# Three mixing products at once, the fourth beside the fifth: the merged loop of a cross-attention and RWKV layer

## The chip, the core and the metric

One core of a Trainium2 chip runs the whole program. The metric is the device time of one execution in microseconds. A profiled execution gives, beside its time, a trace with the start and the duration of each instruction on the engines TensorE (PE), VectorE (DVE), ScalarE (ACT), GpSimd (POOL) and on the queue of SyncE (SP).

## What is computed

The input is x, 64 sequences of 64 rows with 256 channels, and an encoder state of the same shape. First comes a transformer layer (self-attention, cross-attention, MLP), then an RWKV block on its output. All in float32. The part around the change is the token mixing of the RWKV block, cut to what matters:

```python
sx = concatenate([state[:, 1:2] - xa[:, :1], xa[:, :-1] - xa[:, 1:]], axis=1)
xxx = tanh((xa + sx * maa_x) @ maa_w1).reshape(b, l, 5, 32)
xxx = einsum('blfd,fde->blfe', xxx, maa_w2)            # the five mixing products
xm = xa[:, :, None] + sx[:, :, None] * (maa_stack + xxx)
xk, xw, xv, xr, xg = (xm[:, :, j] for j in range(5))
w = exp(-exp(time_decay + tanh(xw @ td_w1) @ td_w2))
r, k, v, g = xr @ Wr.T, xk @ Wk.T, xv @ Wv.T, silu(xg @ Wg.T)
# then for each step t, per head:  out = r (u * k v + s);  s = k v + w s
```

Each of the five mixing products has a contraction of only 32 (`DM`), so it fills a quarter of TensorE's rows.

## The kernel before

The rows are cut into 16 runs of 256 (`RUNS`, `RT`). The late phase is one merged loop over s: in the turn s, TensorE, VectorE, ScalarE and GpSimd each go through a fixed, hand-written order (their `body(s, u)`), in which several stages of different runs stand side by side. Run s is in the recurrence (states, scan, read), run s + 1 in the mixing and its projections, run s + 2 in the first norm, run s + 3 in the transformer's MLP (`up`, `gelu`, `down`), runs s - 1 and s - 2 in the norm of the heads and the output projection. Turns -2 to 3 are written out, 4 to 11 run as a loop on each engine, 12 to 15 are written out again. From s = 13 on there is no MLP run, and two runs of the channel mix (`ch_...`) a turn take its place. The engines meet only at semaphores; each engine works through its own order and a wait holds up all that stands behind it.

The lines around the change:

- TensorE: `mixer` makes the inputs of the five products, ScalarE's `mixer` takes the tanh of them into `mixer_a` (four products, 32 rows each) and `mixer_b` (the fifth, for two column halves, in rows 0 to 31 and 64 to 95). `mix_pair(r, 0)` (matmul on line 1048) makes products 0 and 1 in the banks `even` and `odd`, side by side since they use different rows. After `up(s + 3, 2)` and `up(s + 3, 3)` (line 999), `mix_pair(r, 2)` makes products 2 and 3 in the same banks, once VectorE has read 0 and 1 (`mixed_ready`). `mix_last` (line 1059) makes the fifth, its two column halves side by side in 64 rows each, half of them zeros. `decay` (line 1101) follows it. `project` (lines 1070 for NW, 1089 for the others) makes the projections in the order NW, NV, NK, NR, NG; NW, NV and NG use the bank `proj`, which `up` uses as well; so NW waits until all GELU activations (line 1387) have read it. NK has `k_bank` and NR `r_bank`, which VectorE reads straight from PSUM up to the end of its turn: `project(s, NR)` is the first step of TensorE's turn and waits for VectorE's last `read` (line 1799).
- `sum_heads` (line 1128) sums the heads in `o_bank`, which `add_heads` on VectorE copies out (`o_copied`).
- VectorE: eight groups n = 0 to 7 a turn, each `key_values` (line 1774), `scan` (1788) and `read` (1799; for n = 2 and 3 on GpSimd, line 903). Between them stand the other steps, the mixing among them: `mix(s + 1, m)` (line 1754, two instructions each) takes product m out of PSUM, for m = 0 and 1 after the scan of n = 3, for 2 and 3 after `centre` at n = 4, for 4 after `sum_squares` (line 1837) at n = 5. Product m goes into one of two buffers `mixed`, m modulo 2, so mix m waits until GpSimd has taken mix m - 2 (`xm_ready`).
- GpSimd: `mix(s + 1, m)` (line 894) adds xa to it; in its order stand the reads of n = 2 and 3, mix 0, mix 1, the MLP's bias (`add_mlp_bias`, line 870), mix 2, mix 3, mix 4, then `scale` (line 911).

## Time and profile before

| | us |
|---|---|
| median of 3 runs | 1121.56 |
| lowest and highest | 1116.63, 1121.56 |
| profiled execution, its own time | 1118.86 |
| its span, first to last instruction | 1117.1 |
| mean granted TensorE clock | 0.989 of full |

| engine | busy us | share of the span |
|---|---|---|
| TensorE (PE) | 1061.3 | 95% |
| its weight loads (PEld) | 883.5 | 79% |
| VectorE (DVE) | 916.1 | 82% |
| ScalarE (ACT) | 702.6 | 63% |
| GpSimd (POOL) | 608.1 | 54% |

The attention takes the first 480 us or so, the merged loop the time from there to about 1060. A busy share is a mean over both. A float32 matmul shows as two instructions, so a product of 128x256 counts as x2. TensorE's records overlap: the next one starts before the end of the last, so its time is read from start to start. A duration on VectorE or GpSimd contains the time for which the instruction had been started and yet stood.

### The profile page before, as it was taken

To read this page: it belongs to the slowest core of one execution; us is meant where nothing else is said; L and a number is where in the kernel's file an instruction comes from. 1 tells how busy PE (TensorE), PEld (TensorE's weight loads), DVE (VectorE), ACT (ScalarE), POOL (GpSimd) and SP (SyncE) were. 2 spreads that over 40 slices of the span, in tenths; PEclk is the share of its full clock that TensorE was granted. 3 is DMA by queue.
4 is the path that set the end of the run, shared out by engine and by line. 5 is a ranking of instruction groups with operands and counts; after the bars stand their busy time and mean duration, and the time that the engine had idled before them with its cause. 6 is when DMAs were issued, how large, how long until landed. Compare 5 with 4: busy or idle time off the path is not lost.

```text
span 1117.1 us, 34410 instructions
## 1 busy us (share of the span) xinstructions
PE 1061.3 (95%) x12992; PEld 883.5 (79%) x12992; DVE 916.1 (82%) x1662; ACT 702.6 (63%) x1606; POOL 608.1 (54%) x535
## 2 busy tenths in 40 slices
PE   5999999999999998999999999999999998788898
PEld 4888988888889887777787877777777776566687
DVE  5997777888777776228999999999999999999753
ACT  5678878777777775465556555456555455544574
POOL 4787887877887885024443454443454443444233
PEclk9999999999999998999999999999999999998999
DMA  8500000011111110013333331233331233304011
GB/s 328 174 4 2 0 0 2 3 41 41 41 48 38 38 47 3 1 28 68 79 83 86 85 70 40 64 81 84 84 76 40 56 82 86 85 10 114 20 38 57
DMA packets 39867, 65.01 MB, mean 58 GB/s; under 512 B 4384, under 2 KB 26208, under 8 KB 39392
## 3 DMA queue, kind: packets, MB, share of 16 engines
q1 hardware_dynamic: 39776, 63.75, 21.4%
q8 instruction: 62, 1.02, 0.4%
q14 instruction: 29, 0.24, 0.1%
HBM read 55.35 MB, written 8.39 MB: 57 GB/s over the span
## 4 chain that ended last, share of the span: by engine, by line
PE 60%; DVE 27%; issue 7%; ACT 3%; DVEq 1%; DMA 1%; SPq 0%; POOL 0%; ACTq 0%; POOLq 0%
PE psum L353 9%; DVE shared L1788 9%; PE psum L267 5%; PE psum L999 5%; PE psum L336 5%; PE psum L1008 4%; PE psum L368 4%; PE psum L1089 4%; DVE shared L1774 4%; PE psum L297 4%; PE psum L280 3%; DVE late_mixed L1754 3%; PE psum L1270 2%; PE psum L310 2%; PE psum L1300 2%
## 5 line engine op out<-in xcount | busy, mean ns | idle before, releaser
L1788 DVE TENSOR_TENSOR_SCAN shared<-late_wT,shared 128x512 f32<-128x512 f32 x128 | 192.4, 1503 | 0.0
L232 POOL TENSOR_TENSOR shared<-shared,att_row_max 128x512 f32<-128x512 f32 x128 | 132.3, 1051 | 17.9 <-DVE att_row_max L564 17.9
L353 PE MATMUL psum<-shared 128*128 128x128 f32 x1024 | 126.6, 277 | 0.0
L453 ACT ACTIVATE shared<-shared 128x512 f32<-128x512 f32 x128 | 80.5, 631 | 67.7 <-POOL shared L232 67.6
L353 PEld LDWEIGHTS psum<-shared 128*128 128x128 f32 x1024 | 121.0, 194 | 0.3 <-ACT shared L462 0.2
L999 PE MATMUL psum<-late_glnT,w 128*128 128x256 f32 x512 | 119.5, 387 | 1.8 <-ACT late_glnT L1378 1.8
L1008 PE MATMUL psum<-w,late_hT 128*128 128x256 f32 x512 | 120.0, 383 | 1.0 <-ACT late_hT L1387 0.9
L564 DVE TENSOR_REDUCE att_row_max<-shared 128x8 f32<-128x512 f32 x128 | 86.9, 680 | 40.9 <-POOL shared L225 40.9
L903 POOL TENSOR_TENSOR shared<-shared,late_rT 128x512 f32<-128x512 f32 x32 | 40.7, 1273 | 140.6 <-DVE shared L1788 140.6
L894 POOL TENSOR_TENSOR late_xm<-late_mixed,late_xa 128x512 f32<-128x512 f32 x64 | 79.7, 1255 | 59.9 <-DVE late_mixed L1754 56.3
L999 PEld LDWEIGHTS psum<-late_glnT,w 128*128 128x128 f32 x512 | 95.8, 192 | 17.9 <-issue 2.8
L1008 PEld LDWEIGHTS psum<-w,late_hT 128*128 128x128 f32 x512 | 94.6, 190 | 15.0 <-ACT late_hT L1387 1.8
L225 POOL TENSOR_TENSOR shared<-shared 128x512 f32<-128x512 f32 x64 | 80.0, 1271 | 41.2 <-DVE shared L557 39.5
L225 POOL TENSOR_TENSOR shared<-shared,self_bias 128x512 f32<-128x512 f32 x64 | 80.2, 1275 | 30.7 <-DVE shared L557 30.7
L1387 ACT ACTIVATE late_hT<-psum,cols 128x256 f32<-128x256 f32 x128 | 53.7, 470 | 65.5 <-PE psum L999 65.1
L1774 DVE TENSOR_TENSOR shared<-shared,psum 128x504 f32<-128x504 f32 x128 | 85.6, 670 | 5.7 <-ACT shared L1431 5.6
L267 PEld LDWEIGHTS psum<-shared 64*64 64x64 f32 x4096 | 65.7, 135 | 21.0 <-issue 20.9
L1754 DVE SCALAR_TENSOR_TENSOR late_mixed<-psum,cols,late_sx 128x256 f32<-128x256 f32 x160 | 66.5, 475 | 15.2 <-PE psum L1048 8.3
L462 ACT ACTIVATE shared<-psum 128x512 f32<-128x512 f32 x128 | 68.4, 585 | 7.8 <-PE psum L280 7.8
L267 PE MATMUL psum<-shared 64*64 64x17 f32 x4096 | 72.1, 209 | 0.0
L424 ACT ACTIVATE shared<-psum,cols 128x256 f32<-128x256 f32 x128 | 65.3, 564 | 9.7 <-PE psum L310 6.8
L336 PE MATMUL psum<-shared 128*128 128x128 f32 x512 | 70.3, 282 | 0.4 <-issue 0.4
(168 smaller groups left out, 2420.9 us busy)
## 6 DMA issues: line engine op xcount, KB each, us to landing
shared<-v_rows SPq DMA_DIRECT2D x64, 512.0 KB, 7.1
shared<-in_enc SPq DMA_DIRECT2D x64, 128.0 KB, 2.6
v_rows<-shared SPq DMA_DIRECT2D x64, 64.0 KB, 1.8
out<-x SPq DMA_DIRECT2D x16, 256.0 KB, 2.0
x<-in_x SPq DMA_DIRECT2D x7, 512.0 KB, 9.7
w<-in_w SPq DMA_DIRECT2D x2, 1024.0 KB, 16.9
shared<-in_cross_mask SPq DMA_DIRECT2D x1, 1024.0 KB, 11.4
shared<-in_w_qkv SPq DMA_DIRECT2D x1, 768.0 KB, 4.5
```

Source lines behind the costliest of these rows:

```text
L225: nc.gpsimd.tensor_tensor(zs, zs, bias.unsqueeze(1).to_broadcast([P, PAIRS, S]), ALU.add).then_inc(biased, 1)
L232: nc.gpsimd.tensor_tensor(zs, zs, peak.unsqueeze(2).to_broadcast([P, PAIRS, S]), ALU.subtract).then_inc(shifted, 1)
L267: last = nc.tensor.matmul(out_banks[e ^ b][rows, pair * 32:pair * 32 + HD + 1], zT[keys, pair, rows], values[keys, u, e ^ b, pair, :], sta ...
L336: last = nc.tensor.matmul(vv[:, e * P:(e + 1) * P].rearrange("p (r d) -> p r d", d=HD), KV[k][:, u % 2, kb, e * S:e * S + P], wv[:, kb, v0 ...
L353: last = nc.tensor.matmul(dst[:, half * P:(half + 1) * P], w[:, kb, c0 + half * P:c0 + (half + 1) * P], src[:, u % 2, kb, 0:P], start=(kb ...
L453: nc.scalar.activation(probs[:, u % 2, half * 4:(half + 1) * 4, :].rearrange("p r k -> p (r k)"), z[:, u % 2, half, :], ACT.Exp).then_inc( ...
L564: nc.vector.tensor_reduce(out=row_max[:, u % 2, half * PAIRS:(half + 1) * PAIRS], in_=z[:, u % 2, half, :].rearrange("p (h k) -> p h k", k=S),
L999: last = nc.tensor.matmul(bank[:, (h % 2) * RT:(h % 2 + 1) * RT], w["w1"][:, kb, h * P:(h + 1) * P], glnT[:, kb, :], start=(kb == 0), stop ...
L1008: last = nc.tensor.matmul(mlp[:, c * C:(c + 1) * C], hT[:, h, c * P:(c + 1) * P], w["w2"][:, h, :], start=(h == 0), stop=(h == HIDDEN - 1))
L1754: last = nc.vector.scalar_tensor_tensor(out=mixed[:, m % 2, half, :].rearrange("p (c t) -> p c t", c=CH), in0=products, scalar=col(core, " ...
L1774: nc.vector.tensor_tensor(st[:, n, :, :, 1:S], v_rep[:, n // PER_SUM, n % PER_SUM * JG:(n % PER_SUM + 1) * JG, :].rearrange("p j (b t) -> ...
L1788: nc.vector.tensor_tensor_scan(states, wT[:, u, half, :, :, :].rearrange("p j b t -> p (j b t)"), states, 0.0, ALU.mult, ALU.add).then_inc ...
```

## The change

On TensorE, `mix_three` makes the first three products at once, the third in `o_bank`, and waits for `o_copied` of the run before, since it overwrites the head sums. The pair behind `up` is gone. `mix_two` stands where `mix_last` stood: it makes the fifth (now with 32 rows for each half) and, in the same group, the fourth in the bank `proj`, whose rows are 96 to 127; it waits until ScalarE has copied V out of `proj`. `sum_heads` at q = 0 waits until VectorE has read the third product from `o_bank`, and the projection NG until it has read the fourth from `proj`. On VectorE, mix 2 moves from n = 4, behind `centre`, to n = 3, behind `make_stats`; mix 3 moves from n = 4 to the head of n = 5, before `sum_squares`. The order on GpSimd, ScalarE and SyncE stays.

```diff
--- before.py
+++ after.py
@@ -737,6 +737,7 @@
 
         small, even, odd, proj, o_bank, mlp = (core.banks[i] for i in (3, 4, 5, 2, 0, 1))
         k_bank, r_bank = core.banks[6:8]
+        mix_banks = (even, odd, o_bank, proj)
         decays = core.psum[:, 3 * 512:3 * 512 + 2 * 1280].rearrange("p (c n) -> p c n", c=CH)[:, :, 0:RT]
         fifth = core.psum[:, 4 * 512:6 * 512].rearrange("p (c n) -> p c n", c=CH)[:, :, 0:RT]
 
@@ -1031,35 +1032,38 @@
                                                 xin[:, kb, c * P:(c + 1) * P], start=(kb == 0), stop=(kb == HALVES - 1))
                 last.then_inc(mixer_ready, 1)
 
-            def mix_pair(r, m):
-                if m == 0:
-                    pe.wait_ge(mixer_tanh, r + 1)
-                    if s_is(r, 0):
-                        pe.wait_ge(att.x_ready, att.all)
-                    if later(r):
-                        pe.wait_ge(bonus_v_ready, r)
-                    if later(r - 2):
-                        pe.wait_ge(x_ready, r - 2)
-                else:
-                    pe.wait_ge(mixed_ready, r * NMIX + m)
-                for half in range(HALVES):
-                    for k, bank in ((m, even), (m + 1, odd)):
+            def mix_three(r):
+                pe.wait_ge(mixer_tanh, r + 1)
+                if s_is(r, 0):
+                    pe.wait_ge(att.x_ready, att.all)
+                if later(r):
+                    pe.wait_ge(bonus_v_ready, r)
+                if later(r - 1):
+                    pe.wait_ge(o_copied, r - 1)
+                if later(r - 2):
+                    pe.wait_ge(x_ready, r - 2)
+                for half in range(HALVES):
+                    for k in range(3):
                         rows = slice(MIX[k] * DM, (MIX[k] + 1) * DM)
-                        last = nc.tensor.matmul(bank[:, half * RT:(half + 1) * RT],
+                        last = nc.tensor.matmul(mix_banks[k][:, half * RT:(half + 1) * RT],
                                                 core.maa_w2a[rows, half * P:(half + 1) * P], mixer_a[rows, :],
                                                 start=True, stop=True)
                         if half == HALVES - 1:
                             last.then_inc(mix_ready, 1)
 
-            def mix_last(r):
-                pe.wait_ge(mixed_ready, r * NMIX + NMIX - 1)
+            def mix_two(r):
+                pe.wait_ge(mixed_ready, r * NMIX + 2)
+                pe.wait_ge(copied, r * 3 + NV)
+                fourth = slice(MIX[3] * DM, (MIX[3] + 1) * DM)
                 for half in range(HALVES):
                     for c, bank in enumerate((even, odd)):
-                        rows = slice(c * DD, (c + 1) * DD)
-                        last = nc.tensor.matmul(bank[:, half * P:(half + 1) * P],
-                                                core.maa_w2b[rows, c, half * P:(half + 1) * P],
-                                                mixer_b[rows, :], start=True, stop=True)
-                last.then_inc(mix_ready, 1)
+                        rows = slice(c * DD, c * DD + DM)
+                        nc.tensor.matmul(bank[:, half * P:(half + 1) * P], core.maa_w2b[rows, c, half * P:(half + 1) * P],
+                                         mixer_b[rows, :], start=True, stop=True)
+                    last = nc.tensor.matmul(proj[:, half * RT:(half + 1) * RT],
+                                            core.maa_w2a[fourth, half * P:(half + 1) * P], mixer_a[fourth, :],
+                                            start=True, stop=True)
+                last.then_inc(mix_ready, 2)
 
             def project(r, m):
                 pe.wait_ge(xm_ready, r * NMIX + m + 1)
@@ -1076,6 +1080,7 @@
                     pe.wait_ge(decay_tanh, r + 1)
                 elif m == NG:
                     pe.wait_ge(copied, r * 3 + NV)
+                    pe.wait_ge(mixed_ready, r * NMIX + 4)
                 elif later(r):
                     pe.wait_ge(copied, (r - 1) * 3 + m)
                     if m == NK:
@@ -1122,6 +1127,8 @@
                     pe.wait_ge(read_ready, r * (GROUPS_R - PER_SUM) + (q + 1 - int(q > POOL_SUM)) * PER_SUM)
                 if q == 0 and later(r):
                     pe.wait_ge(o_copied, r)
+                if q == 0 and there(r + 1):
+                    pe.wait_ge(mixed_ready, (r + 1) * NMIX + 3)
                 for jl in range(JQ):
                     rows = slice(jl * RH, (jl + 1) * RH)
                     states = st[:, q * PER_SUM + jl // JG, jl % JG, :, :].rearrange("p b t -> p (b t)")
@@ -1189,7 +1196,7 @@
                     up(s + 3, 0)
                     up(s + 3, 1)
                 if mixing:
-                    mix_pair(s + 1, 0)
+                    mix_three(s + 1)
                 if early(s):
                     ch_transpose(early_run(s, 1), 1)
                 if old:
@@ -1200,7 +1207,6 @@
                 if early(s):
                     ch_keys(early_run(s, 0), 0)
                 if mixing:
-                    mix_pair(s + 1, 2)
                     project(s + 1, NW)
                 if now:
                     sum_heads(s, 0)
@@ -1212,7 +1218,7 @@
                 if mlp_run:
                     down(s + 3, 0)
                 if mixing:
-                    mix_last(s + 1)
+                    mix_two(s + 1)
                     decay(s + 1)
                 if early(s):
                     ch_values(early_run(s, 0), 0)
@@ -1750,7 +1756,7 @@
                     if m == NMIX - 1:
                         products = fifth[:, :, half * P:(half + 1) * P]
                     else:
-                        products = (even, odd)[m % 2][:, half * RT:(half + 1) * RT].rearrange("p (c t) -> p c t", c=CH)
+                        products = mix_banks[m][:, half * RT:(half + 1) * RT].rearrange("p (c t) -> p c t", c=CH)
                     last = nc.vector.scalar_tensor_tensor(
                         out=mixed[:, m % 2, half, :].rearrange("p (c t) -> p c t", c=CH), in0=products,
                         scalar=col(core, "maa_stack", MIX[m] * HALVES + half),
@@ -1952,17 +1958,18 @@
                         mix(s + 1, 1)
                     if n == 3 and there(s - 2) and not s_is(s, RUNS - 1):
                         make_stats(s - 2)
+                    if n == 3 and there(s + 1):
+                        mix(s + 1, 2)
                     if s_is(s, RUNS - 4) and n == 4:
                         ch_variances(0)
                     if n == 4:
                         if there(s - 1) and not s_is(s, RUNS - 1):
                             centre(s - 1, 1 - u)
-                        if there(s + 1):
-                            mix(s + 1, 2)
-                            mix(s + 1, 3)
                         if early(s):
                             ch_mix(early_run(s, 1), 1)
                     if n == 5:
+                        if there(s + 1):
+                            mix(s + 1, 3)
                         if early(s):
                             ch_finish(early_run(s, 0), 0)
                         if there(s - 1) and not s_is(s, RUNS - 1):
```

## Rows read from the trace of the kernel before

**Rows 1.** Busy by stretch: length, PE, PEld, DVE, ACT, POOL; clock, DMA, GB/s.

```profile
538.00:569.20 31.20, 31.20 (x200) 24.48 (x200) 30.79 (x48) 17.75 (x40) 14.77 (x12) 1.00 0.33 77
770.20:803.70 33.50, 33.46 (x210) 26.30 (x209) 33.01 (x52) 18.69 (x42) 14.82 (x11) 1.00 0.31 72
939.00:978.00 39.00, 29.96 (x191) 22.40 (x191) 37.22 (x62) 21.00 (x47) 16.10 (x13) 1.00 0.28 66
```

**Rows 2.** Timeline, TensorE: start us, us, what; NR of s = 2 and s = 12.

```profile
566.53 1.95 PE L1089 MATMUL psum<-late_xm,WrT 128*128 128x256 f32 x8
...
901.62 1.97 PE L1089 MATMUL psum<-late_xm,WrT 128*128 128x256 f32 x8
```

**Rows 3.** Timeline, TensorE: around NR at s = 0, and at s = 8.

```profile
504.04 1.89 PE L1008 MATMUL psum<-w,late_hT 128*128 128x256 f32 x8
505.77 1.89 PE L1089 MATMUL psum<-late_xm,WrT 128*128 128x256 f32 x8
...
765.63 1.89 PE L1008 MATMUL psum<-w,late_hT 128*128 128x256 f32 x8
767.50 1.99 PE L1089 MATMUL psum<-late_xm,WrT 128*128 128x256 f32 x8
```

**Rows 4.** Timeline, TensorE: one loop turn from the second pair to the next NR.

```profile
785.99 1.13 PE L1048 MATMUL psum<-late_mixer_a,maa_w2a 32*128 32x256 f32 x8
787.05 0.66 PE L1070 MATMUL psum<-late_xm,td_w 128*64 128x128 f32 x8
...
792.29 0.71 PE L1059 MATMUL psum<-late_mixer_b,maa_w2b 64*128 64x128 f32 x8
792.84 0.61 PE L1101 MATMUL psum<-late_decay_in,td_w 64*128 64x128 f32 x8
793.38 3.72 PE L1008 MATMUL psum<-w,late_hT 128*128 128x256 f32 x16
...
799.11 1.89 PE L1008 MATMUL psum<-w,late_hT 128*128 128x256 f32 x8
801.04 1.99 PE L1089 MATMUL psum<-late_xm,WrT 128*128 128x256 f32 x8
802.87 0.60 PE L985 MATMUL psum<-ident,late_gxn 128*128 128x128 f32 x4
```

**Rows 5.** Timeline, VectorE: the same turn from n = 4 to the last read.

```profile
784.50 0.66 DVE L1774 TENSOR_TENSOR shared<-shared,psum 128x504 f32<-128x504 f32 x1
785.08 2.00 DVE L1788 TENSOR_TENSOR_SCAN shared<-late_wT,shared 128x512 f32<-128x512 f32 x1
...
791.26 2.20 DVE L1788 TENSOR_TENSOR_SCAN shared<-late_wT,shared 128x512 f32<-128x512 f32 x1
...
794.10 1.06 DVE L1837 TENSOR_REDUCE late_moments<-shared 128x64 f32<-128x512 f32 x1
795.06 0.88 DVE L1754 SCALAR_TENSOR_TENSOR late_mixed<-psum,cols,late_sx 128x256 f32<-128x256 f32 x2
...
796.43 1.85 DVE L1788 TENSOR_TENSOR_SCAN shared<-late_wT,shared 128x512 f32<-128x512 f32 x1
...
798.92 1.34 DVE L1788 TENSOR_TENSOR_SCAN shared<-late_wT,shared 128x512 f32<-128x512 f32 x1
800.29 0.69 DVE L1799 TENSOR_TENSOR shared<-shared,psum 128x512 f32<-128x512 f32 x1
```

**Rows 6.** Timeline, ScalarE: the last two GELU activations, with the idle time before.

```profile
786.10 0.84 ACT L1387 ACTIVATE late_hT<-psum,cols 128x256 f32<-128x256 f32 x2 [0.89 <-PE psum L999]
```

**Rows 7.** The scan line (ns min/median/max); timeline, GpSimd: mix 0, 1 and bias.

```profile
L1788 DVE TENSOR_TENSOR_SCAN shared<-late_wT,shared x128: 1210/1220/2217, 507.2 to 1039.9; 128x512 f32<-128x512 f32 x128
...
783.68 2.32 POOL L894 TENSOR_TENSOR late_xm<-late_mixed,late_xa 128x512 f32<-128x512 f32 x2
785.95 2.20 POOL L870 TENSOR_TENSOR x<-x,rows 128x512 f32 x1
```

**Rows 8.** Timeline, VectorE: the channel mix at s = 13.

```profile
961.28 2.96 DVE L1892 SCALAR_TENSOR_TENSOR late_hT<-shared,cols 128x256 f32<-128x256 f32 x4
```

## The prediction

> **What bounds the kernel now.** The page puts TensorE at 95% and VectorE at 82% of the span, shares over stages that differ, so I read the busy time by stretch first. In one turn of the merged loop TensorE is busy 33.46 us of 33.5 and VectorE 33.01 [rows 1]: both look full, and busy time alone doesn't say which one sets the pace. The places where each waits do. From the start of one `project(s, NR)` to that ten turns later there are (901.62 - 566.53)/10 = 33.51 us a turn [rows 2]. Where TensorE waits for nothing, eight matmul instructions take 1.73 us (504.04 to 505.77), 0.216 us each [rows 3]. In the loop the eight ahead of NR take 1.93 us (799.11 to 801.04) and the eight of NR 1.83 (to 802.87) [rows 4]: 0.30 us of waiting. A turn earlier the first of the two takes 1.87 (765.63 to 767.50) [rows 3], so 0.24; 0.27 on average. What ends this wait is VectorE's last read of `r_bank`, over at 800.29 + 0.69 = 800.98 [rows 5]. I found no other wait of TensorE in the turn, so its own work is 33.51 - 0.27 = 33.24 us, and VectorE sets the pace by just that. In the turns before the loop (s = -1, 0, 1) TensorE is busy 31.20 of 31.20 us [rows 1] and waits nowhere at NR [rows 3]: there it is the bound itself. In the last turns (s = 12, 13, 14) VectorE is, with 37.22 of 39.0 us against 29.96 [rows 1].
>
> **The second pair goes.** It takes 785.99 to 787.05, 1.06 us [rows 4]. What follows it is `project(s + 1, NW)`, which waits for the whole GELU. The last two GELU activations end at 786.10 + 0.84 = 786.94 [rows 6], and NW starts 0.11 us later. They read what the last `up` made just before the pair, so the pair lies wholly inside the way from TensorE to ScalarE and back. Without it TensorE stands idle from 785.99 until the same 787.05. Gain: 0. This decides the case, and it holds in each turn with an MLP run (s = -1 to 12).
>
> **The third product joins the first pair.** A pair has 8 instructions in 1.06 us: four steps of 0.216 (0.86) with two side by side, and 0.20 for going into 32-row tiles and out of them. A third product in rows of its own costs between 0 and 0.86 (its four steps alone). I take 0.02, since of the two in the pair the second costs nothing that the row shows.
>
> **The fourth goes beside the fifth.** Now the fifth takes 792.29 to 792.84, 0.55 us, and the decay product behind it 0.54, to 793.38 [rows 4]; both use 64-row tiles. Afterwards one product of the group is 256 columns wide, which makes the group as long as a pair, 1.06, and the decay product has to go into 64-row tiles anew, 0.10 (half of the pair's 0.20). Sum 1.06 + 0.54 + 0.10 = 1.70 instead of 1.09: +0.61. Lower bound +0.42 (the width alone: 0.86 less four steps of 0.11), upper bound +1.06 (nothing overlaps). I take 0.61, built from the pair, the row nearest to it.
>
> The Trainium skill (TensorE: Matmul & The Clock Gate, section Measured speedup vs the span model) prices a pack of tiles as one matmul's duration and about 4 ns for each further tile. The pair's row has 0.20 us beyond its four steps that this rule doesn't name; by the rule alone the new group would cost no more than its width, and the whole change would come out at +0.7 us.
>
> **TensorE's new turn**: 33.24 + 0.02 + 0.61 = 33.87 us.
>
> **VectorE.** A scan alone takes 1.22 us [rows 7]. Four of the eight in a turn take 2.00, 2.20, 1.85 and 1.34 [rows 5]: 0.78 + 0.98 + 0.63 + 0.12 = 2.51 us in which they stand until an instruction of GpSimd is over. GpSimd's bias instruction, which takes 2.20 where its neighbours take 1.16 each, shows the same from the other side [rows 7]. The moved steps shift this:
> - `mix(s + 1, 2)` now comes where the n = 4 product starts, at 784.50 [rows 5], and has to wait for GpSimd's mix 0 (783.68 + half of 2.32 = 784.84 [rows 7], and some 0.08 until it is seen): +0.43. All of VectorE's queue waits behind it.
> - Mix 2 takes 0.78 and the product 0.58, so the n = 4 scan starts at 786.29. It meets the bias instruction, begun at 785.95, about 1.2 long alone: 0.70 instead of 0.78.
> - The n = 5 scan meets an idle GpSimd, since GpSimd's mix 3 now follows that scan: 0 instead of 0.98.
> - n = 6 and 7 keep their distance to mix 4: unchanged.
>
> Together -0.63: VectorE's own turn is 32.88, below TensorE's 33.87, so TensorE becomes the bound. One new wait could undo this: mix 3 on VectorE now needs the products of `mix_two`. It would come at 794.10 - 0.78 + 0.43 - 0.08 - 0.98 = 792.69, while they are there 1.06 + 0.13 after 792.29, at 793.48: 0.8 us of standing. From the start of `mix_two` VectorE then needs 1.19, 0.78 for mix 3, 0.96 for the squares, 5.92 (795.06 to 800.98) up to its last read [rows 5], and 0.05 until TensorE sees it: 8.90. TensorE itself needs 801.04 - 792.29 less its wait of 0.20, and 0.61 more: 9.16. VectorE is early by 0.26.
>
> The other new waits stand on TensorE's queue, with everything behind them, and are covered. `o_copied` before `mix_three` comes from `add_heads` at n = 2, a step ahead of mix 0, which wants the products. `mixed_ready` + 3 before `sum_heads(s, 0)` is there by 785.8, before NW at 787.05. `copied` before `mix_two` has `down(s + 3, 0)`, 1.73 us, between V's projection and it. `mixed_ready` + 4 before NG is asked for in the next turn. The decays end 0.61 later, yet mix 3 and the squares now hold mix 4 up longer than that. No DMA moves.
>
> **Sum.** Ten loop turns at 33.87 - 33.51 = 0.36: +3.6. Three TensorE-bound turns before them at 0.63: +1.9. Three last turns, VectorE-bound: -0.63 at s = 12; at s = 13 and 14 four channel-mix instructions take 2.96 us beside GpSimd [rows 8], against some 1.7 alone, and GpSimd will be done by then: -1.2 + 0.43 - 0.1 = -0.87 each; -2.4 in all. Net +3.1 us, or 13x - 4.8 with x the price of the fourth product. The profiled execution took 1118.86 (span 1117.1 and 1.8 around it), so 1122.0 on its scale. The median of the runs shown is 2.7 higher, 1121.56; on that scale I say **1124.7**.
>
> **Rivals.**
> - *Faster*: the idle 1.06 us isn't paid, as the GELU would end sooner. TensorE then needs 32.8 and VectorE's 32.88 sets the turn: -6.3 in the loop, -1.3 before, -2.4 behind: 1111.6. Against it: NW starts 0.11 after the GELU's end already now, and nothing moves that end. 0.09.
> - *Slower*: the fourth product runs after the fifth and not beside it, their widths being unequal, of which no row has an example. x = 1.06: +9.0, 1130.6; it counts as slower from x = 0.80 on. For it: each change of tile height costs 0.1 already. Against it: equal widths overlap fully. 0.13.
> - *The end gives nothing back*, since channel work and GpSimd interlock otherwise there: +5.5, 1127.1. 0.12.
> - *It doesn't do what it says*: the third product runs behind the pair, 0.86 in 13 turns, 11.2 more: 1135.9. 0.03.
> - The forecast: 0.63, from 1118 to 1128 by itself.
>
> A measurement of this kernel can tell about 0.5%, 5.6 us, from no change: faster is under 1116.0, slower over 1127.2. Faster 0.09, the first rival. Slower 0.25: the second, the fourth, half of the third and the forecast's own end. Same 0.66. The range of 1116 to 1131 leaves out the first and the fourth rival.
>
> **What would show it.** After the change: TensorE idle about 1.07 us before NW in each loop turn, ended by the GELU; turns of 33.9; no wait before NR; the group of three 1.06 long and the decay product 0.64; on VectorE the n = 5 scan at 1.22, a wait for GpSimd before mix 2 and one for TensorE before mix 3. I am wrong if NW starts right behind `up`, if the turn is at or below 33.5, or if the group of `mix_two` takes over 1.3 us.

## The result, and the profile after

The changed kernel takes 1122.31 us (median of ten runs, 1119.79 to 1125.49), the kernel before 1119.56 beside it (ten runs, 1116.63 to 1121.82). The ratio is 1.0027, with an interval of 1.0014 to 1.004: slower, by an amount inside the 0.5% band that the prediction calls no change. The profiled execution of the changed kernel took 1121.93 us (span 1120.1, mean granted clock 0.991) against 1118.86 (1117.1, 0.989), so +3.1 us in time and +3.0 in the span, where the prediction has +3.1. By the medians it is 1122.31 - 1119.56 = 2.75.

The page of the changed kernel, its busy times and the shares of the chain that ended last:

```profile
span 1120.1 us, 34440 instructions
PE 1050.8 (94%) x12992; PEld 876.4 (78%) x12992; DVE 905.6 (81%) x1662; ACT 701.7 (63%) x1606; POOL 607.2 (54%) x535
...
PE 80%; DVE 10%; issue 4%; ACT 4%; POOL 1%; DMA 0%; DVEq 0%; ACTq 0%; POOLq 0%
```

TensorE is busy 10.5 us less than before and the kernel is longer: part of the work went out of a place that has to be waited through anyway. In the kernel before, the same chain lay to 60% on TensorE and to 27% on VectorE. It lies to 80% and 10% there now, so TensorE has become the bound.

The changed kernel by stretch, with the columns of [rows 1]:

```profile
538.00:569.20 31.20, 29.89 (x194) 23.38 (x193) 29.32 (x46) 17.67 (x40) 14.79 (x11) 1.00 0.23 54
771.20:805.00 33.80, 32.87 (x210) 26.03 (x209) 32.31 (x52) 18.59 (x42) 14.80 (x11) 1.00 0.30 69
940.90:979.10 38.20, 29.32 (x190) 21.88 (x189) 36.23 (x62) 19.15 (x43) 15.90 (x13) 1.00 0.36 83
```

In a loop turn TensorE is busy 32.87 us of 33.8, so idle 0.93, where it was idle 0.04 of 33.5 [rows 1]. VectorE has fallen from 33.01 to 32.31. The same turn on TensorE, start and duration, cut to one NR, the stretch from the group of three to the next NR, and the transposes behind it:

```profile
771.26 1.89 PE L1094 MATMUL psum<-late_xm,WrT 128*128 128x256 f32 x8
...
784.54 1.14 PE L1048 MATMUL psum<-late_mixer_a,maa_w2a 32*128 32x256 f32 x12
...
786.10 3.62 PE L1000 MATMUL psum<-late_glnT,w 128*128 128x256 f32 x16
790.65 0.66 PE L1074 MATMUL psum<-late_xm,td_w 128*64 128x128 f32 x8 [0.93 <-ACT late_hT L1393]
...
795.89 0.38 PE L1061 MATMUL psum<-late_mixer_b,maa_w2b 32*128 32x128 f32 x2
...
796.44 0.59 PE L1063 MATMUL psum<-late_mixer_a,maa_w2a 32*128 32x256 f32 x2
796.96 0.71 PE L1106 MATMUL psum<-late_decay_in,td_w 64*128 64x128 f32 x8
797.61 3.72 PE L1009 MATMUL psum<-w,late_hT 128*128 128x256 f32 x16
...
803.33 1.89 PE L1009 MATMUL psum<-w,late_hT 128*128 128x256 f32 x8
805.06 1.89 PE L1094 MATMUL psum<-late_xm,WrT 128*128 128x256 f32 x8
806.78 0.60 PE L986 MATMUL psum<-ident,late_gxn 128*128 128x128 f32 x4
```

- The turn is 805.06 - 771.26 = 33.80 us.
- Where the pair stood [rows 4], TensorE now stands 0.93 us until the GELU is over. From the start of `up`'s last block to NW it takes 790.65 - 786.10 = 4.55 us. In the kernel before, with the pair in it, that block starts at 782.44 (below) and NW at 787.05 [rows 4], so 4.61.
- The last GELU ends at 789.76 + 0.84 = 790.60 (below), and NW starts 0.05 us later; before it was 0.11.
- The group of `mix_two` takes 796.96 - 795.89 = 1.07 us and the decay product 0.65, together 1.72 instead of the 1.09 of [rows 4].
- The eight instructions ahead of NR take 1.73 us and those of NR 1.72: as in the unwaited place of [rows 3]. The 0.27 us of waiting for VectorE's last read are gone.

`up`'s last block on TensorE in the kernel before, and the last GELU on ScalarE in the changed one:

```profile
782.44 3.62 PE L999 MATMUL psum<-late_glnT,w 128*128 128x256 f32 x16
```

```profile
789.76 0.84 ACT L1393 ACTIVATE late_hT<-psum,cols 128x256 f32<-128x256 f32 x2 [0.89 <-PE psum L1000]
```

The same turn on VectorE, which answers to [rows 5]:

```profile
788.58 0.88 DVE L1760 SCALAR_TENSOR_TENSOR late_mixed<-psum,cols,late_sx 128x256 f32<-128x256 f32 x2 [0.40 <-POOL late_xm L895]
789.37 0.67 DVE L1780 TENSOR_TENSOR shared<-shared,psum 128x504 f32<-128x504 f32 x1
789.95 1.97 DVE L1794 TENSOR_TENSOR_SCAN shared<-late_wT,shared 128x512 f32<-128x512 f32 x1
...
794.54 1.22 DVE L1794 TENSOR_TENSOR_SCAN shared<-late_wT,shared 128x512 f32<-128x512 f32 x1
...
797.07 0.88 DVE L1760 SCALAR_TENSOR_TENSOR late_mixed<-psum,cols,late_sx 128x256 f32<-128x256 f32 x2 [0.59 <-PE psum L1063]
...
800.20 1.85 DVE L1794 TENSOR_TENSOR_SCAN shared<-late_wT,shared 128x512 f32<-128x512 f32 x1
```

The scan of n = 5 has fallen from 2.20 to 1.22 us. Mix 2 now waits 0.40 for GpSimd's mix 0, and mix 3 waits 0.59 for the products of `mix_two`.

Where the 3.07 us of the span lie (1117.07 and 1120.15 to the hundredth), from the starts of NR in both traces:

| part | before | after | difference |
|---|---|---|---|
| up to the first NR (s = 0) | 505.77 | 505.82 | +0.05 |
| the turns s = 0 and 1 | 29.67, 31.10 | 30.31, 32.09 | +1.64 |
| ten turns, s = 2 to 11 | 335.09 | 338.24 | +3.15 |
| s = 12, 13, 14 | 34.75, 38.77, 37.93 | 34.43, 38.18, 37.37 | -1.47 |
| from the last NR to the end | 104.01 | 103.72 | -0.29 |

The first row hides two things. From the first mixing product of the merged loop to the first NR, which is the rest of the turn s = -1, the kernel before takes 505.77 - 486.69 = 19.08 us and the changed one 505.82 - 486.11 = 19.71, so this turn pays 0.63 as well. What stands ahead of it, the attention above all, was 0.58 us shorter in this execution. In the traces of all the runs below the first mixing product starts at 483.9 to 487.4 and the last NR is 102.9 to 104.7 from the end, with no order by kernel, so the first and the last row can't be told from chance. TensorE's timeline, before and after:

```profile
486.69 1.13 PE L1048 MATMUL psum<-late_mixer_a,maa_w2a 32*128 32x256 f32 x8
```

```profile
486.11 1.14 PE L1048 MATMUL psum<-late_mixer_a,maa_w2a 32*128 32x256 f32 x12
...
505.82 1.89 PE L1094 MATMUL psum<-late_xm,WrT 128*128 128x256 f32 x8
```

### The profile page after: what moved, and what is told of

The parts are those of the page before. It is cut to its first block, busy times and chain, and to the rows that moved or that the text cites. A ratio compares the mean times of both kernels' runs of the same rounds, so it can differ in the third digit from the quotient of the medians.

```text
span 1120.1 us, 34440 instructions
## 1 busy us (share of the span) xinstructions
PE 1050.8 (94%) x12992; PEld 876.4 (78%) x12992; DVE 905.6 (81%) x1662; ACT 701.7 (63%) x1606; POOL 607.2 (54%) x535
## 4 chain that ended last, share of the span: by engine, by line
PE 80%; DVE 10%; issue 4%; ACT 4%; POOL 1%; DMA 0%; DVEq 0%; ACTq 0%; POOLq 0%
PE psum L353 10%; PE psum L1009 9%; PE psum L1000 9%; PE psum L1094 8%; PE psum L267 6%; PE psum L336 5%; PE psum L368 5%; PE psum L297 4%; PE psum L280 3%; DVE shared L1794 3%; PE psum L1135 2%; PE psum L310 2%; PE psum L1276 2%; PE psum L1306 2%; PE psum L1168 2%
## 5 line engine op out<-in xcount | busy, mean ns | idle before, releaser
L1794 DVE TENSOR_TENSOR_SCAN shared<-late_wT,shared 128x512 f32<-128x512 f32 x128 | 180.8, 1413 | 0.0
L895 POOL TENSOR_TENSOR late_xm<-late_mixed,late_xa 128x512 f32<-128x512 f32 x64 | 75.0, 1181 | 100.0 <-DVE late_mixed L1760 100.0
```

The lines of the kernel that those rows point to most:

```text
L1794: nc.vector.tensor_tensor_scan(states, wT[:, u, half, :, :, :].rearrange("p j b t -> p (j b t)"), states, 0.0, ALU.mult, ALU.add).then_inc ...
```

## The experiments

The theory: TensorE's stretch between `up` and NW has a fixed length, which the GELU sets; what is done in it is free, and what is moved out of it is paid. The rivals were VectorE as the bound of the changed kernel, and the GELU coming sooner. Medians of the kernel before stand beside each set: 1119.44 us (29 runs) for the first four, 1120.32 (17 runs) for the next four, 1118.59 (11 runs) for the last.

### The pair left out of the kernel before

```diff
-                            last.then_inc(mix_ready, 1)
+                            last.then_inc(mix_ready, 1 if k == 0 else 3)
...
-                    mix_pair(s + 1, 2)
```

> The kernel before with the second pair (products 2 and 3) left out: VectorE reads what lies in the two banks, so x for K and R is not the reference's; all other work and waits stay. My theory (the pair lay inside the GELU's round trip and cost TensorE nothing): TensorE idles some 1.06 us before NW in each turn, NW starts about 0.12 us after the GELU's end as before, turns stay at 33.5 us, and the time stays that of the kernel before (1119.6, within 1 us). Rival (the pair was a cost of TensorE's turn): TensorE's own turn shrinks by 1.06, its 0.3 wait at NR grows to about 1.3, and the time falls where TensorE was the bound, by 3 us or more (three turns of 1.06).

Measured: 1118.23 us, ratio 0.9989 (0.9974 to 1.0003). The turns stay at 33.4 to 33.6. TensorE's timeline in this kernel, at the place of [rows 4]:

```profile
781.97 3.62 PE L999 MATMUL psum<-late_glnT,w 128*128 128x256 f32 x16
786.51 0.66 PE L1070 MATMUL psum<-late_xm,td_w 128*64 128x128 f32 x8 [0.93 <-ACT late_hT L1386]
```

With the pair gone and nothing put elsewhere, `up` to NW is still 786.51 - 781.97 = 4.54 us, and the 1.06 us of the pair have turned into 0.93 of idle time (the records of neighbours overlap by 0.07, and the stretch is 0.07 shorter). The plainest proof lies in the turns s = 0 and 1, where TensorE is the bound and a gain on it would show in full: they take 29.68 and 31.10 us, where the kernel before has 29.67 and 31.10. So removing the pair gains nothing there, and the rival in which the GELU ends sooner is out. The median is 1.2 us below that of the kernel before beside it, a little more than the 1 us expected; the interval holds 1, so it shows no gain either.

### The changed kernel without its fourth product

```diff
-                    last = nc.tensor.matmul(proj[:, half * RT:(half + 1) * RT],
-                                            core.maa_w2a[fourth, half * P:(half + 1) * P], mixer_a[fourth, :],
-                                            start=True, stop=True)
```

> The changed kernel without the fourth product: the group of mix_two holds the fifth alone (32 rows), VectorE's mix 3 reads what V's projection left in the bank, so R is not the reference's. My theory (the fourth's width is what TensorE pays for): the group takes about 0.55 instead of 1.07 and the decay product 0.65, so x falls from 0.63 to about 0.1, TensorE's own turn from 33.80 to about 33.3, mix 3 stops waiting, and the time falls by 13 x 0.5 = 6.5 us or somewhat less, to about 1116. Rival (the time of the change comes from VectorE's moved steps and new waits, not from TensorE): turns stay at 33.8 and the time at 1122.

Measured: 1117.04 us, ratio 0.998 (0.9965 to 0.9995); seven of the ten turns s = 2 to 11 take 33.37, which is 33.80 - 0.43. TensorE's timeline in this kernel:

```profile
794.75 0.71 PE L1061 MATMUL psum<-late_mixer_b,maa_w2b 32*128 32x128 f32 x8
795.39 0.71 PE L1103 MATMUL psum<-late_decay_in,td_w 64*128 64x128 f32 x8
796.04 3.72 PE L1009 MATMUL psum<-w,late_hT 128*128 128x256 f32 x16
```

The fifth product alone, in 32-row tiles, and the decay take 0.64 + 0.65 = 1.29 us. That splits the 0.63 us in two. 1.29 - 1.09 = 0.20 is the price of the order of tile heights: TensorE goes from 128 rows to 32, to 64 and back to 128, one change more than the 128, 64 and 128 of before. 1.72 - 1.29 = 0.43 is the price of the width of the fourth. It is four steps of 0.216 less four of 0.11, as worked out for the lower bound: inside the group the fifth costs nothing beside the fourth, though their widths differ.

The turn s = 2 is an exception, with 35.31 us. VectorE waits 1.19 us there for V's rows, and TensorE then 0.51 and 1.03 us for VectorE. With TensorE faster, the transfer of V's rows is the next thing to be waited for in the first turns.

The Trainium skill (TensorEngine Tiling (Array Packing), section Key Properties) says that changing the tiling mode drains TensorE. This trace agrees in that one change more takes 0.20 us more; that the time is spent in draining is not shown by it.

### The idle time filled with other work

`transpose_o` and the first `sum_heads`, which stood elsewhere in the order, go between `up` and NW.

```diff
-                if old:
+                if old and not mlp_run:
                     transpose_o(s - 1)
...
+                if old and mlp_run:
+                    transpose_o(s - 1)
+                if now and mlp_run:
+                    sum_heads(s, 0)
                 if mixing:
                     project(s + 1, NW)
```

> The changed kernel, with two steps of TensorE moved into the idle time before NW: transpose_o from ahead of the third up to behind the fourth (0.49 us), and the first sum_heads from behind NW to ahead of it (0.50 us). Nothing is left out. My theory (1.06 us idle per turn before NW): the idle time shrinks to about 0.1, TensorE's own turn falls to about 32.8, VectorE's 32.9 becomes the bound, NR's wait comes back small; turns of about 33.0 us. 0.8 x 10 + 1 x 2 less than the changed kernel, so about 1112, 0.7% faster than the kernel before. Rival (the idle time only shows where TensorE waits for something slower that would then show elsewhere): turns stay at 33.5 to 33.8, time 1119 to 1122.

Measured: 1119.2 us, ratio 0.9997 (0.9982 to 1.0013). Of the turns s = 2 to 11 seven take 33.24 to 33.33 and three 33.80 to 33.97, not 33.0, and the whole is 7 us worse than expected. Something took a part of the gain. TensorE's timeline, then ScalarE's:

```profile
793.33 0.38 PE L1061 MATMUL psum<-late_mixer_b,maa_w2b 32*128 32x128 f32 x2 [0.28 <-ACT shared L1450]
```

```profile
792.05 0.63 ACT L1485 ACTIVATE shared<-shared 128x512 f32<-128x512 f32 x1 [2.90 <-DVE shared L1838]
792.70 0.58 ACT L1450 ACTIVATE shared<-psum 128x512 f32<-128x512 f32 x1
```

`mix_two` waits for ScalarE's copy of V out of `proj`. ScalarE is free, yet the copy stands in its order behind the square, and the square has waited 2.90 us for VectorE's `centre`. So TensorE depends on VectorE's pace over ScalarE's order, and `mix(s + 1, 2)` ahead of `centre` makes `centre` late. It is the wait whose cover the prediction had named as `down(s + 3, 0)`, about 1.8 us. In the changed kernel VectorE is through with `centre` 1.79 us after V's projection begins, which the cover holds; with TensorE earlier it is 2.61 us. At s = 0 and 1 the filled order costs more than it gives: the head sums, now ahead of NW, wait 1.63 and 0.75 us there until VectorE has read the third product, and the turn s = 0 takes 31.04 instead of 30.31.

### Mix 2 back behind `centre`

```diff
-                    if n == 3 and there(s + 1):
-                        mix(s + 1, 2)
...
                             centre(s - 1, 1 - u)
+                        if there(s + 1):
+                            mix(s + 1, 2)
```

> The changed kernel with VectorE's mix 2 back at its old place, behind centre at n = 4; nothing left out. It tells what that move was worth. By the trace of after, mix 2 would be done about 22.2 us after NR begins, while TensorE wants to begin the head sums (which overwrite product 3) at 20.1: TensorE would stand about 2 us per turn before the first sum_heads; turns near 35.8 us, time near 1122 + 13 x 2 = 1148. VectorE's new wait for GpSimd (0.40) goes, and its n = 5 scan stands again (0.6). Rival (the order on VectorE doesn't matter, the head sums come late enough): within 3 us of 1122.

Measured: 1190.29 us, ratio 1.0616 (1.0585 to 1.0648). The loop turns are mostly 37.6 to 37.9, one is 39.26; 35.8 was expected. TensorE's timeline in the long one, then the busy time by stretch around it:

```profile
821.48 0.66 PE L1074 MATMUL psum<-late_xm,td_w 128*64 128x128 f32 x8 [0.93 <-ACT late_hT L1393]
824.47 1.93 PE L1135 MATMUL psum<-shared,head_sum 128*32 128x256 f32 x16 [2.34 <-DVE late_mixed L1760]
826.33 3.78 PE L1094 MATMUL psum<-late_xm,WvT 128*128 128x256 f32 x8
```

```profile
815.00:821.40 6.40, 5.55 (x35) 4.09 (x33) 6.40 (x11) 2.49 (x6) 4.51 (x4) 1.00 0.00 0
821.40:824.40 3.00, 0.66 (x8) 0.42 (x8) 2.93 (x8) 0.93 (x3) 1.18 (x1) 0.93 0.00 0
824.40:832.00 7.60, 7.53 (x32) 5.11 (x32) 3.05 (x4) 1.98 (x4) 1.19 (x1) 0.58 0.00 0
832.00:839.00 7.00, 7.00 (x46) 5.75 (x45) 5.61 (x9) 4.98 (x12) 4.11 (x3) 1.00 0.63 153
```

The head sums now need the third product read out of `o_bank`, and wait 2.34 us for it: as expected, in mechanism and about in size (a turn of 35.8 was 2.0 more). The rest is the clock. After TensorE was busy 0.66 us of 3.00, the granted clock is 0.58 of full over the next 7.6 us, so most of that stretch runs at the lower level, 1.2 GHz instead of 2.4, and then it is back at 1.00. From NW to `mix_two` it takes 10.70 us instead of 5.24. Of these 5.46, the wait is 2.34; the head sums take 0.86 more than in the changed kernel, V's projection 1.75 more and the `down` behind it 0.45 more. In the turns of 37.8 the lower level lasts less long (V's projection takes 2.37 us in one of them, and 3.58 here); why it varies is open. The three last turns grow by 5.9, 6.7 and 6.5 us; in two of them the head sums wait 3.52 and 4.41 us.

This shows what the early place of mix 2 is for: with the third product in the head sums' bank, VectorE has to read it before `sum_heads(s, 0)`, or each loop turn costs 4 us more.

### Mix 2 between the product and the scan of n = 4, in the changed kernel

```diff
+                    if n == 4 and there(s + 1):
+                        mix(s + 1, 2)
+                    if there(s):
                         scan(s, u, n)
...
-                    if n == 3 and there(s + 1):
-                        mix(s + 1, 2)
```

> The changed kernel with VectorE's mix 2 put between the product and the scan of n = 4; nothing left out. By the trace of after, its wait for GpSimd (0.40) goes, and the scan behind it starts just after GpSimd's mix 1 is over, so it stands 0 to 0.1 instead of 0.75: VectorE's own turn is 1.1 us shorter. My theory (TensorE alone sets the loop's turn after the change): loop turns stay at 33.80, VectorE only waits longer for TensorE; what falls is the VectorE-bound end, up to 1.1 in each of three turns, so 1119 to 1121. Rival (VectorE's new waits are part of the turn): turns fall below 33.5 and the time by 8 us or more.

Measured: 1122.16 us, ratio 1.0021 (1.001 to 1.0033): what the changed kernel itself has (1.0027), and not the 1119 to 1121 us expected. VectorE's timeline:

```profile
787.36 0.87 DVE L1760 SCALAR_TENSOR_TENSOR late_mixed<-psum,cols,late_sx 128x256 f32<-128x256 f32 x2
788.15 1.22 DVE L1794 TENSOR_TENSOR_SCAN shared<-late_wT,shared 128x512 f32<-128x512 f32 x1
...
795.75 0.88 DVE L1760 SCALAR_TENSOR_TENSOR late_mixed<-psum,cols,late_sx 128x256 f32<-128x256 f32 x2 [1.83 <-PE psum L1063]
```

The order does what it was made for. Mix 2 doesn't wait, the scan of n = 4 takes 1.22 instead of 1.97, and VectorE is 1.2 us ahead. It loses the whole lead again at mix 3, which waits 1.83 us for TensorE instead of 0.59, and the turn stays at 33.80. In the loop TensorE alone sets the time. The last turns hardly move either (34.32, 38.18 and 37.39 after 34.43, 38.18 and 37.37; up to 1.1 less was expected in each), so VectorE's lead doesn't set them any more.

### Both together, and the square behind the copy

This is the filled kernel with mix 2 moved as in the last one, and on ScalarE `square(s - 1)` behind its copies.

```diff
-                if there(s - 1) and not s_is(s, RUNS - 1):
-                    square(s - 1)
...
                         set_states(s + 1, 1)
+                if there(s - 1) and not s_is(s, RUNS - 1):
+                    square(s - 1)
```

> The kernel `filled` with two more moves: VectorE's mix 2 between the product and the scan of n = 4 (as in after_mix2), and on ScalarE the square of the centred heads behind the copy of V instead of ahead of it. In the trace of filled, TensorE waits 0.21 to 0.28 for the copy of V, which stands behind that square, which waits for VectorE's centre (issued late); VectorE waits 0.38 for GpSimd and stands 0.76 in the n = 4 scan. My theory (in filled both engines are bound, coupled over the copy of V): turns fall from 33.3 to about 33.0, TensorE's own work, and the end gives 1.1 for each of three turns: about 1113. Rival (V's way over DRAM has become the bound, as the waits for v_rows in turns 1 and 2 hint): turns stay at 33.3 and VectorE's wait before its first product names the DMA; time 1116 to 1119.

Measured: 1112.94 us, ratio 0.9947 (0.9933 to 0.9962). Eight of the turns s = 2 to 11 take 32.98, the first two 33.07, and a stretch of one turn shows:

```profile
764.30:797.30 33.00, 33.00 (x209) 26.03 (x208) 31.50 (x52) 18.58 (x42) 14.80 (x11) 1.00 0.30 70
```

TensorE has no idle time left in the loop, and VectorE is 1.5 us below it. The rival, V's rows as the bound, is out. The time is the 1113 expected, but not by the expected parts: the three last turns together are only 0.4 us shorter than in the filled kernel, where 1.1 was expected of each.

### Both together, with the square where it was

The same without the change on ScalarE, so that against the filled kernel only mix 2 is moved:

```diff
+                    if n == 4 and there(s + 1):
+                        mix(s + 1, 2)
+                    if there(s):
                         scan(s, u, n)
...
-                    if n == 3 and there(s + 1):
-                        mix(s + 1, 2)
```

> The kernel `filled` with only VectorE's mix 2 moved. If the coupling over ScalarE is real, VectorE reaches centre 1.1 us earlier, the square with it, and the copy of V is no longer held up: nearly the same as filled_all, turns of 33.0. Rival (ScalarE's order matters by itself): turns stay at 33.2 to 33.3, and only the end of the kernel is faster, 1116.

Measured: 1114.88 us, ratio 0.9955 (0.9937 to 0.9972); seven of the turns s = 2 to 11 take 32.98, the first two 33.07 and one 33.20. Moving mix 2 alone is thus enough in the loop: with `centre` earlier, the square no longer holds up the copy. That confirms the coupling read in the filled kernel: TensorE waits for the copy three times in the whole kernel, and 14 times there. The two kernels' times overlap (1110.8 to 1115.6 and 1113.32 to 1116.4), so what the order on ScalarE adds stays open.

### The kernel before, with its mixing ahead of `centre`

```diff
                     if n == 4:
-                        if there(s - 1) and not s_is(s, RUNS - 1):
-                            centre(s - 1, 1 - u)
                         if there(s + 1):
                             mix(s + 1, 2)
                             mix(s + 1, 3)
+                        if there(s - 1) and not s_is(s, RUNS - 1):
+                            centre(s - 1, 1 - u)
```

> The kernel before with one thing moved on VectorE: mix 2 and mix 3 ahead of centre at n = 4 instead of behind it. No product moves on TensorE. GpSimd's mix 3 is then over before the n = 5 scan starts, which should take 1.22 instead of 2.20: VectorE's own turn 32.5. My theory (VectorE sets the turn of the kernel before by 0.27, TensorE's own work being about 33.2): turns fall from 33.51 to about 33.2, the end by up to 1 us in each of three turns: 1114 to 1117. Rival (33.5 is set by something both share): turns stay at 33.5, time 1117 to 1120.

Measured: 1114.25 us, ratio 0.9955 (0.9941 to 0.9969); turns of 33.23 to 33.27. VectorE's scan of n = 5 in this kernel:

```profile
790.21 1.22 DVE L1788 TENSOR_TENSOR_SCAN shared<-late_wT,shared 128x512 f32<-128x512 f32 x1
```

TensorE's timeline around the NR behind it:

```profile
798.10 1.89 PE L1008 MATMUL psum<-w,late_hT 128*128 128x256 f32 x8
799.83 1.89 PE L1089 MATMUL psum<-late_xm,WrT 128*128 128x256 f32 x8
```

One changed place in VectorE's order, with TensorE's order untouched, takes the collision of the n = 5 scan away and gives 0.5%. The instructions ahead of NR take 799.83 - 798.10 = 1.73 us, so nothing is waited for there any more: the turn of 33.23 is TensorE's own, which the prediction had worked out as 33.24. The change under study contains the same gain on VectorE, and then spends more than that on TensorE.

This is also the measure for the filled kernels. Their ratios, 0.9947 and 0.9955, can't be told from this 0.9955. The packing and the filling bring the loop turn from 33.23 to 32.98, 2.4 us over ten turns, and lose 1.3 and 0.5 us of it in the turns s = 0 and 1.

### The best of both

The filled order (with mix 2 in front of the scan and the square behind) in the turns 2 to 12 only; before and behind them the pairs of the kernel before, mix 2 and 3 ahead of `centre`.

```diff
+        def packed(s):
+            return not isinstance(s, int) or FIRST_PACKED <= s <= LAST_PACKED
...
                 if mixing:
-                    mix_three(s + 1)
+                    if packed(s):
+                        mix_three(s + 1)
+                    else:
+                        mix_pair(s + 1, 0)
...
-                    mix_two(s + 1)
+                    if packed(s):
+                        mix_two(s + 1)
+                    else:
+                        mix_last(s + 1)
```

> `filled_all` in the turns s = 2 to 12 alone; in the written-out turns before and after them the order of the kernel before, with mix 2 and 3 ahead of centre as in before_mix_first. Nothing is left out. In the turns 0 and 1 filled_all takes 31.05 and 31.63 us where before_mix_first takes 29.70 and 31.10; in the last two 38.27 and 37.39 against 38.10 and 36.72. If the products packed in three only pay where an MLP run gives work to move into the idle time and a `down` hides the copy of V, the hybrid keeps 32.98 in the loop and takes the lower of the two at both ends: 1.9 and 0.8 us less than filled_all, about 1110. Rival (the turns at the ends are coupled to the loop's, so that what is won there is waited for again): the time of filled_all, 1113.

Measured: 1110.97 us (1108.23 to 1114.1), ratio 0.9921 (0.9895 to 0.9946). The first turns are 29.68 and 31.1, those of the kernel before, and the loop's 32.98. In the profiled execution, at 1114.1 the longest of its six, the last turn took 39.9 us with the clock lower in it. The turn s = 14 takes 36.72 in the kernel before with its mixing ahead of `centre`, whose order this kernel has there. The version is faster than both kernels of the study, by 0.8% against the one before. It has the lowest median of all, but whether it is faster than the filled kernel with both changes (0.9947, interval 0.9933 to 0.9962) the overlapping intervals leave open; the first turns came out as expected, the last one didn't.

## Why the prediction was right, step by step

**The second pair costs nothing: right, and the heart of the case.** The idle time before NW is 0.93 us by the row and ended by the GELU, in the changed kernel and in the kernel before without its pair. What made this readable ahead was one distance: NW began 0.11 us after the last GELU. The turns s = 0 and 1, unchanged without the pair, show the same in time.

**The third product costs nothing: right.** The group of three takes 785.61 - 784.54 = 1.07 us (the second number is where the next operation starts), the pair 1.06.

**The fourth costs 0.61: right, 0.63.** By parts it was 0.43 for the width and 0.20 for the tile changes, where the prediction took 0.51 (1.06 less 0.55) and 0.10. The split looks wrong, but the 0.51 holds tile changes too: 1.06 is four steps of 0.216 and 0.20 of them, 0.55 is four steps of 0.11 and 0.11 of them. So 0.42 of the 0.51 is width and 0.09 is tile changes, 0.19 with the other 0.10, and both agree with the measured parts. The Trainium skill (TensorE: Matmul & The Clock Gate, section Measured speedup vs the span model), by which the price would have been the width alone, 0.42, gives the part for the width well; the measured sum is 0.2 higher.

**TensorE's turn of 33.87: measured 33.80.** From its own turn before, 33.23, come 0.63 + 0.01 for the groups and 4.61 - 4.55 = 0.06 less before NW, 33.81. The prediction had NW start at the same 787.05 without the pair, that is 0.11 us after the GELU. In the eight turns written as a loop it now starts 0.05 after it, in the changed kernel and in the one before without its pair alike: there the pair had held NW up by 0.06 us, which come back. In the written-out turns s = 2 and 3 NW starts 0.14 us after the GELU with the pair and without it, and nothing comes back; why these turns differ from the loop is open. The 0.09 us between 4.64 and 4.55 are most of why they take 33.91 and not 33.80. Ten turns at 33.80 would give +2.9, these two add 0.2, and that makes the +3.15 measured for +3.6.

**VectorE falls below it: right.** The wait for GpSimd was 0.40 (predicted 0.43), the excess of the n = 4 scan 0.75 (0.70), of the n = 5 scan 0 (0). Mix 3 stood 0.59 instead of 0.8, and VectorE was no longer late at NR. The reading behind these terms, that a scan stands until GpSimd's instruction is over, is borne out in both directions: with the order changed and the work the same, the scan returns to 1.22 in the kernel before, and GpSimd's bias instruction to 1.27 in the changed one, as this row of its timeline has it, while the mix 2 behind it meets the scan of n = 4 and takes 2.12:

```profile
789.57 1.27 POOL L871 TENSOR_TENSOR x<-x,rows 128x512 f32 x1
790.79 2.12 POOL L895 TENSOR_TENSOR shared<-late_mixed,late_xa 128x512 f32<-128x512 f32 x1
```

The Trainium skill (SBUF — State Buffer, section Who interferes with whom) says that a VectorE instruction with two SBUF inputs contends with a GpSimd instruction that reads SBUF, over ports that are an exclusive lock, and that the order of issue decides which of the two stands. The rows agree: in the changed kernel the scan of n = 4 starts at 789.95, 0.38 us behind the bias instruction, and takes 1.97, while the mix 2 of GpSimd starts at 790.79 behind that scan and takes 2.12.

**The waits called covered: right in the loop, wrong at its edges.** `copied` before `mix_two` had a `down` in front of it in my argument, and there is no `down` where there is no MLP run. TensorE's timeline of the changed kernel, at s = 13, in time order:

```profile
960.10 0.66 PE L1074 MATMUL psum<-late_xm,td_w 128*64 128x128 f32 x8 [1.72 <-POOL late_xm L895]
961.17 1.07 PE L1135 MATMUL psum<-shared,head_sum 128*32 128x256 f32 x16 [0.41 <-DVE late_mixed L1760]
...
966.77 0.38 PE L1061 MATMUL psum<-late_mixer_b,maa_w2b 32*128 32x128 f32 x2 [0.88 <-ACT shared L1445]
```

It waits 0.88 there for ScalarE's copy and again at s = 14, 0.47 at s = 12, where a `down` does stand in front, and 0.29 at s = 1. The `sum_heads` wait for `mixed_ready` + 3 costs 0.41. NW waits 1.72 us for GpSimd's mix 0, since without an MLP run there is no GELU to wait for; but that is no new loss, for in the kernel before the second pair stood in the same place, behind a wait of 0.79 us, and the stretch from `ch_keys` to NW was 3.82 us long and is 3.69 now. With these waits and the 0.63 of `mix_two`, the channel's products come so late that VectorE waits 0.33 us for them at s = 13, where it didn't wait before. At s = 12 the turn is no longer VectorE's: it is TensorE's 33.80, the 0.47 of waiting and 0.09 for a later NW. So the step that was mis-sized is the end of the loop as bound by VectorE alone: -2.4 predicted (-0.63, -0.87, -0.87), -1.47 measured (-0.32, -0.59, -0.56). The gain of the channel mix, 2.96 to 1.67 us, was there as predicted, and a part of it was lost in these waits:

```profile
965.29 1.67 DVE L1898 SCALAR_TENSOR_TENSOR late_hT<-shared,cols 128x256 f32<-128x256 f32 x4
...
970.52 0.69 DVE L1906 SCALAR_TENSOR_TENSOR w<-w,psum 128x512 f32<-128x512 f32 x1 [0.33 <-PE psum L1306]
```

The wait for the pair in the kernel before, at the same s = 13, on TensorE:

```profile
954.73 1.13 PE L1048 MATMUL psum<-late_mixer_a,maa_w2a 32*128 32x256 f32 x8 [0.79 <-DVE late_mixed L1754]
```

**"No DMA moves": not quite.** VectorE waits for V's rows in the turns s = 2 and 3, 0.29 and 0.28 us, and it waited nowhere for them before:

```profile
568.18 0.68 DVE L1780 TENSOR_TENSOR shared<-shared,psum 128x504 f32<-128x504 f32 x1 [0.29 <-DMA shared<-v_rows]
```

The trace of before shows no wait there, and so I hadn't asked how near to one it was. In the changed kernel without its fourth product the wait at the same place was 1.19 us, and reached TensorE. In the changed kernel it doesn't seem to: the turns s = 2 and 3 are explained but for 0.03 us by NW's later start.

**The turns before the loop: right, and a little more.** Three TensorE-bound turns at 0.63 were +1.9 predicted. They gave 0.63 at s = -1, 0.65 at s = 0 and 0.99 at s = 1, which has the wait of 0.29 us at `mix_two` in it: +2.27. Against it stands an attention 0.58 us shorter, which leaves the +0.05 and +1.64 of the table.

The sum came out as +3.07 for +3.1. The prediction had 0.45 us too much in the loop, 0.4 too little in the turns before it and 0.9 too little at the end, which together would have made 3.9; a start shorter by 0.58 and a tail shorter by 0.29, neither of them predicted, took it back to 3.1. The mechanism was right, and that the sum agrees to a tenth is luck. The absolute 1124.7 was 2.4 over the measured 1122.31: 2.0 of it because it stood on a median of three runs, 1121.56, which ten runs put at 1119.56.

## What to carry to other kernels

Before counting an instruction's time as gained, look at what the next instruction on its engine waits for: if that event isn't moved, the instruction is free where it stands, and moving its work elsewhere costs its full price there. The better use of such a place is the reverse, to bring other work into it, as the filled kernels did; here that was worth 0.25 us a turn. Look first at how two engines stand in each other's way: moving two steps in VectorE's order gave as much as packing and filling together. A wait is covered only in the turns in which the covering step exists: go through the first and last turns of a software pipeline by themselves, and follow each semaphore through the order of the engine that gives it, since a free engine can stand behind a step that waits for a third.

## What the runs showed of the hardware

- **Tiles side by side.** A group of three 32-row products takes what two take (1.07 and 1.06 us), and products of unequal width run side by side too, the group being as long as its widest.
- **Tile height.** Making the fifth product in 32-row tiles ahead of the decay product's 64-row tiles costs 0.20 us more than making both in 64-row tiles (1.29 against 1.09). It is one change of height more.
- **VectorE and GpSimd.** A scan of 128x512 takes 1.22 us alone and 1.34 to 2.20 when a GpSimd instruction was under way at its start. The time stood through is part of the duration and doesn't show as idle.
- **The clock.** TensorE idle 0.93 us in each turn left the granted clock at 1.00 (the stretch 771.20 to 805.00). With 2.34 us more of idle time 0.66 us behind the first, it was 0.58 over the next 7.6 us, and a turn grew by about 4 us, one by 5.46. That a wait can cost more than its length was the largest thing that the expectations had missed.
